# Both layer norms' linear part in TensorE's moving matrix, and three experts on the first half of the tokens ahead of the second

## The reference

```
# layer 0, per token; W, b, emb are picked by the sample's domain id
hidden = gelu(x @ down_W.T + down_b)                   # 32 wide
hidden = hidden @ expert_W[id].T + expert_b[id] + domain_emb[id]
x = layernorm(hidden @ up_W.T + up_b + x) * ln_gamma + ln_beta
# layer 1
h = layernorm(x) * ln_g + ln_b                         # over the features
h = (h - mean over tokens) * rsqrt(var over tokens + 1e-8)
gamma, beta = style(subject id)                        # four small products, softplus
h = h * gamma + beta
gates = the two largest of softmax(h @ router_w), normalised    # 8 experts
y = sum over e of gate_e * (relu(h @ w1_e + b1_e) @ w2_e + b2_e)  # 512 wide
out = x + y
```

## Time and profile before

| | |
|---|---|
| runs | 126.09, 122.81, 125.94 us; median 125.94 |
| profiled execution | 122.93 us; span of its instructions 121.1 us |
| TensorE busy | 114.2 us (94%), 515 matmuls |
| VectorE busy | 93.1 us (77%) |
| ACT busy | 86.6 us (71%) |
| POOL busy | 54.3 us (45%) |
| first expert product | 21.24 us |
| last expert product | 115.41 us |

### The profile page before, as it was taken

One profiled execution on the slowest core, in us unless ns is written; L12 is line 12 of the kernel. 1 busy time (PEld: TensorE's weight loads), 2 busy tenths in 40 slices (PEclk: granted clock), 3 DMA queues, 4 the chain that ended last, 5 costly groups with the idle time before them and its releaser, 6 DMA issues.

```text
span 121.1 us, 1653 instructions
## 1 busy us (share of the span) xinstructions
PE 114.2 (94%) x515; PEld 86.5 (71%) x515; DVE 93.1 (77%) x238; ACT 86.6 (71%) x147; POOL 54.3 (45%) x75
## 2 busy tenths in 40 slices
PE   6999889999859999999999999999999999999990
PEld 2557533888548888788888888888888888888780
DVE  4756999999996699895867777685959577776871
ACT  2157596589789996978778787878787876878300
POOL 5200986420594001100089997948577940312300
PEclk9999756999999999999999999999999999999999
DMA  1998599990000005065999100000000000000006
GB/s 64 374 221 341 138 438 449 349 349 16 0 3 0 0 0 173 8 184 133 345 431 425 54 0 0 5 0 0 0 0 0 0 0 0 5 0 0 0 0 173
DMA packets 4328, 14.17 MB, mean 117 GB/s; under 512 B 544, under 2 KB 1888, under 8 KB 4064
## 3 DMA queue, kind: packets, MB, share of 16 engines
q1 hardware_dynamic: 2880, 9.67, 22.4%
q0 software_dynamic: 1008, 3.67, 8.9%
q10 hardware_dynamic: 432, 0.73, 1.7%
HBM read 13.52 MB, written 0.56 MB: 116 GB/s over the span
## 4 chain that ended last, share of the span: by engine, by line
PE 73%; DVE 21%; issue 2%; ACT 1%
PE bank L577 21%; PE bank L578 20%; PE bank L616 11%; PE bank L596 11%; PE bank L621 4%; DVE hid_low L990 3%; DVE x L887 2%; DVE h_full L969 2%; DVE stats L894 1%; DVE h_low L975 1%; DVE z L931 1%; PE bank L548 1%; DVE bank L879 1%; DVE t_stats L915 1%; DVE stats L846 1%
## 5 line engine op out<-in xcount | busy, mean ns | idle before, releaser
L491 ACT ACTIVATE hid_high<-bank,early_sb 128x512 fp32r<-128x512 f32 x64 | 44.3, 692 | 16.1 <-PE bank L596 16.0
L990 DVE TENSOR_TENSOR hid_low<-bank,hid_high 128x512 fp32r<-128x512 f32 x51 | 34.6, 687 | 18.8 <-ACT bank L494 18.3
L494 ACT ACTIVATE bank<-bank,early_sb 128x512 f32<-128x512 f32 x51 | 33.5, 658 | 0.0
L301 POOL TENSOR_TENSOR w_low<-w_raw,w_high 128x256 fp32r<-128x256 f32 x32 | 23.0, 743 | 12.1 <-ACT w_high L479 6.1
L616 PE MATMUL bank<-hid_low,w_high 128*128 128x512 f32 x64 | 25.6, 399 | 1.5 <-DVE hid_low L990 1.3
L577 PE MATMUL bank<-h_high,w_low 128*128 128x512 f32 x64 | 25.6, 400 | 0.7 <-ACT h_high L473 0.7
L577 PE MATMUL bank<-hid_high,w_low 128*128 128x512 f32 x64 | 25.7, 402 | 0.0
L578 PE MATMUL bank<-h_high,w_high 128*128 128x512 f32 x64 | 25.3, 396 | 0.0
L596 PE MATMUL bank<-h_low,w_high 128*128 128x512 f32 x64 | 25.1, 394 | 0.0
L578 PE MATMUL bank<-hid_high,w_high 128*128 128x512 f32 x64 | 25.0, 391 | 0.0
L311 POOL TENSOR_TENSOR y_sum<-y_sum,y_part 128x512 f32<-128x512 f32 x9 | 11.6, 1291 | 19.0 <-DVE y_part L1010 16.9
(11 more groups left out here) (136 smaller groups left out, 110.3 us busy)
## 6 DMA issues: line engine op xcount, KB each, us to landing
w_high<-w_all_dram POOLq DMA_DIRECT2D x7, 512.0 KB, 6.9
w_raw<-w_all_dram SPq DMA_DIRECT2D x1, 3072.0 KB, 10.9
gate_all<-gate_scratch SPq DMA_DIRECT2D x4, 512.0 KB, 5.5
gate_all<-gate_scratch SPq DMA_DIRECT2D x1, 2048.0 KB, 11.4
w_raw<-w_all_dram SPq DMA_DIRECT2D x2, 512.0 KB, 7.8
style_sb<-style_dram SPq DMA_DIRECT2D x1, 324.0 KB, 4.8
tables_sb<-tables_dram ACTq DMA_DIRECT2D x1, 272.0 KB, 3.0
xT_sb<-xT_dram SPq DMA_DIRECT2D x1, 256.0 KB, 3.6
```

Source lines behind the costliest of these rows:

```text
L301: nc.gpsimd.tensor_tensor(w_low[:, e % W_RING, quarter(q)], w_raw[:, e, quarter(q)], w_high[:, e % W_RING, quarter(q)].bitcast(F32), ALU.s ...
L491: ac(hid_high[:, slot, :], hid_ps[slot][:, :], ACT.Relu, bias=bias).then_inc(relu_steps, 1)
L494: ac(hid_ps[slot][:, :], hid_ps[slot][:, :], ACT.Relu, bias=bias).then_inc(relu_steps, 1)
L990: v.tensor_tensor(low, ps, high.bitcast(F32), ALU.subtract).then_inc(low_vector, 1)
```

## The change

The moving matrix of `residual` and `up` becomes 256 wide (`moments`). Its first 127 columns give a vector whose squares add up to 128 times the variance of the sum; column 127 gives the covariance with beta; the last 128 give the centred sum times gamma. So a sum comes out of PSUM centred and scaled. ACT squares and adds up the first part (`energies`), VectorE takes statistics of the last part and works out from both, in small steps of one column a tile, what the variance of the second norm will be (`sum_var`, `token_var`), without the finished x1. One pass (`shifted`) adds beta times the root. The second norm reads that; x1 itself is made by POOL later (`adapter_out`).

The matrix is built on the chip: POOL makes its constant parts and puts gamma, beta and the up bias, loaded as columns, on diagonals; TensorE multiplies, ACT copies. The up matrix is transposed, multiplied by `moments` (`build_up`) and then by the selected expert (`adapter`), a half at a time, and VectorE copies it (`take_adapter`).

For half 1 POOL takes the roots as powers. ACT loads one table less for Sqrt and one less for Exp; `w_high` of expert 0 comes by a load and not from ACT. POOL normalises one tile each of samples 0 and 1 and both of samples 2 and 3; the statistics over tokens stay with VectorE. Expert 2 on half 0 stands ahead of half 1, so 12 units do instead of 8; the gates are transposed at unit 20 instead of 18. The warm products change from 10 at the start and 5, 6, 3, 2 in the head to 6, 2 and 6, 2, 2.

Of the order lists the new order is shown; the old one stands in the functions above.

```diff
-PRE_ORDER = [(0, 0), (1, 0), (0, 1), (1, 1), (2, 0), (2, 1)]
-WARM_LOAD, WARM_NORM = 10, (5, 6, 3, 2)
-FEATURE_ROOT = 4
+PRE_ORDER = [(0, 0), (1, 0), (2, 0), (0, 1), (1, 1), (2, 1)]
+SECOND = PRE_ORDER.index((0, 1)) * FC
+WARM_LOAD, WARM_BUILD, WARM_NORM = 6, 2, (6, 2, 2)
...
+            sp.dma_start(ln0_cols[:, :], ln_row.rearrange("a b d -> d (a b)"), allow_slow_non_contiguous=True
+                         ).then_inc(ln0_cols_loaded, 16)
             sp.dma_start(xT_sb[:, 0:HN], xT[:, 0:HN]).then_inc(x_loaded[0], 16)
+            up_b_at = EARLY.at["up_b"][0]
+            sp.dma_start(up_b_col[:, :], early[A:A + 1, up_b_at:up_b_at + D].rearrange("a d -> d a"),
+                         allow_slow_non_contiguous=True).then_inc(up_b_loaded, 16)
+            sp.dma_start(xT_sb[:, HN:N], xT[:, HN:N]).then_inc(x_loaded[1], 16)
+            sp.dma_start(style_sb[:, 0:STYLE_FIRST], style[:, 0:STYLE_FIRST]).then_inc(style_loaded, 16)
...
+            sp.dma_start(w_raw[:, 2, :], w_all[:, 2, :]).then_inc(w_loaded[2], 16)
+            sp.dma_start(w_raw[:, 3:E, :], w_all[:, 3:E, :]).then_inc(w_loaded[3], 16)
...
+            pool.wait_ge(ln0_cols_loaded, 16)
+            nc.gpsimd.tensor_scalar(gain_rows[:, 1:1 + D], ident[:, :], ln0_cols[:, 0:1], None, ALU.mult
+                                    ).then_inc(gain_rows_ready, 1)
+            nc.gpsimd.tensor_scalar(gain_rows[:, 0:1], ln0_cols[:, 1:2], ln0_cols[:, 0:1], 1.0 / D, ALU.mult, ALU.mult
+                                    ).then_inc(gain_rows_ready, 1)
+            pool.wait_ge(up_b_loaded, 16)
+            for b in range(HB):
+                nc.gpsimd.tensor_copy(up_b_rows[:, b * SLOT + A:b * SLOT + A + 1], up_b_col[:, :]).then_inc(up_b_ready, 1)
...
+            def normalise(b, tiles):
+                pool.wait_ge(sum_taken, T * (b + 1))
+                pool.wait_ge(mean1_ready, b + 1)
+                if b < HB:
+                    pool.wait_ge(rstd1_ready, b + 1)
+                else:
+                    pool.wait_ge(rstd1_power, b - HB + 1)
+                for j in (b * T + t for t in tiles):
+                    nc.gpsimd.tensor_scalar(z[:, j, :], x1_std[:, j, :], mean1[:, j:j + 1], rstd1[:, j:j + 1],
+                                            ALU.subtract, ALU.mult).then_inc(z_pool, 1)
...
+            def token_rstd(b):
+                js = slice(b * T, (b + 1) * T)
+                pool.wait_ge(var1_ready, b + 1)
+                nc.gpsimd.tensor_tensor(rstd1[:, js], var1[:, js], roots_of[:, 1, :], ALU.pow).then_inc(rstd1_power, 1)
...
+            load_high(0)
             load_high(1)
-            split_lows(0)
-            normalise(0)
-            split_lows(1, (0, 1))
+            normalise(0, (1,))
+            normalise(1, (1,))
+            split_lows(0, (0, 1))
+            pool.wait_ge(pool_steps, steps.n)
+            feature_rstd(0)
+            split_lows(0, (2, 3))
             load_high(2)
             load_high(3)
-            pool.wait_ge(affine_ready, HB)
+            sum_std(2)
+            sum_std(3)
+            token_rstd(2)
+            normalise(2, range(T))
+            split_lows(1, (0, 1))
+            token_rstd(3)
+            normalise(3, range(T))
             split_lows(1, (2, 3))
             load_high(4)
             load_high(5)
-            normalise(2)
-            for q in POOL_UNITS:
-                split_hidden(q)
+            split_lows(2, (0, 1))
+            feature_rstd(1)
+            split_lows(2, (2, 3))
             pool.wait_ge(affine_ready, B)
-            split_lows(2)
             split_lows(3)
+            adapter_out()
...
+            act.dma_start(ids_i[:, :], ids).then_inc(ids_loaded, 16)
             act.dma_start(tables_sb[:, :, :], tables).then_inc(tables_loaded, 16)
             act.dma_start(early_sb[:, :], early).then_inc(early_loaded, 16)
-            act.dma_start(xT_sb[:, HN:N], xT[:, HN:N]).then_inc(x_loaded[1], 16)
...
+            ac(moments[:, K_DIFF:2 * D], gain_ps, ACT.Copy).then_inc(gain_ready, 1)
+            act.wait_ge(up_T_in_psum, 1)
+            ac(up_T[:, :], up_T_ps, ACT.Copy).then_inc(up_T_ready, 1)
+            act.wait_ge(up_moments_in_psum, 1)
+            ac(up_moments[:, :], up_moments_ps, ACT.Copy).then_inc(up_moments_ready, 1)
...
+                    act.wait_ge(sum_in_psum, j + 1)
+                    if b >= HB:
+                        act.wait_ge(stats_ready, T * (b + 1))
+                    elif t > 0:
+                        act.wait_ge(stats_ready, T * b + 1)
+                    ac(z[:, j, 0:K_DIFF], sum_ps[j][:, 0:K_DIFF], ACT.Square, accum_out=energy[:, j:j + 1]
+                       ).then_inc(energy_ready, 1)
...
+            energies(0)
+            sum_std(0)
             act.wait_ge(style_in_psum, 4)
             ac(sty1_T[:, :], sty1_ps, ACT.Relu, bias=col(C_SB1, SC)).then_inc(style_ready, 1)
+            energies(1)
+            token_std(0)
+            sum_std(1)
             act.wait_ge(style_in_psum, 6)
             ac(gamma_raw[:, :], gam_ps, ACT.Identity, bias=col(C_SBG)).then_inc(gamma_beta_ready, 1)
             ac(beta_T[:, :], bet_ps, ACT.Identity, bias=col(C_SBB)).then_inc(gamma_beta_ready, 1)
+            token_std(1)
             softplus()
+            energies(2)
+            energies(3)
             round_h(0)
+            for q in range(9):
+                relu_unit(q)
             round_h(1)
...
+            build_gain()
+            warm(WARM_BUILD, misc[1])
+            up_bias(0)
+            transpose_up()
+            down(0)
+            build_up()
+            down(1)
+            down(2)
+            down(3)
+            adapter(0)
             residual(0)
+            up(0)
+            up_bias(1)
+            adapter(1)
             mm(se_ps, STYLE.of(style_sb, "subj", SUBJ), onehot_s[:, :], start=True, stop=True).then_inc(style_in_psum, 1)
             residual(1)
             up(1)
...
             residual(2)
             pe.wait_ge(style_ready, 2)
+            up(2)
             pe.wait_ge(style_ready, 3)
+            residual(3)
+            pe.wait_ge(style_end_loaded, 16)
             pe.wait_ge(style_ready, 4)
             transpose_z(0)
+            up(3)
             pe.wait_ge(soft_in, 1)
             transpose_z(1)
+            warm(WARM_NORM[0], bank[3])
+            pe.wait_ge(t_rstd_ready, 1)
+            warm(WARM_NORM[1], bank[3], S)
+            pe.wait_ge(affine_ready, HB)
             warm(WARM_NORM[2], bank[3], S)
+            pe.wait_ge(h_even_rounded, 1)
+            pe.wait_ge(h_odd_rounded, 1)
...
+            for q in range(3):
                 first_highs(q)
             pe.wait_ge(h_ready, 1)
+            for q in range(3):
                 first_low(q)
             first_product(3)
+            second_product(0)
+            first_product(4)
             pe.wait_ge(sum_taken, T * HB + T)
             router(0)
+            second_product(1)
             first_product(5)
+            second_product(2)
+            first_product(6)
+            second_product(3, between=lambda: transpose_z(2))
+            first_product(7)
+            second_product(4)
+            first_product(8)
             transpose_z(3)
+            second_product(5)
+            for q in range(9, SECOND):
                 first_product(q)
                 second_product(q - LEAD)
+            def first_of_second_half():
+                pe.wait_ge(h_even_rounded, HALVES)
+                pe.wait_ge(h_odd_rounded, HALVES)
+                first_highs(SECOND)
+            second_product(SECOND - LEAD, between=first_of_second_half)
             pe.wait_ge(h_ready, HALVES)
...
+            def take_adapter(h):
+                ve.wait_ge(up_eff_in_psum, h + 1)
+                v.tensor_copy(up_eff[:, h, :], up_eff_ps[:, h, :]).then_inc(up_eff_ready, 1)
...
+            def sum_var(b):
+                last = v.tensor_scalar(var0[:, js], energy[:, js], 1.0 / D, LN_EPS, ALU.mult, ALU.add)
+                if b < HB:
                     last.then_inc(vec_steps, steps.add())
+                    own()
                 else:
+                    last.then_inc(var0_ready, 1)
+                    own()
+                    ve.wait_ge(var0_ready, b - HB + 1)
                 for j in tiles(b):
+                    v.scalar_tensor_tensor(cov[:, j:j + 1], mv[:, j, 0:1], minus_shift[:, 0:1], sum_ps[j][:, K_DIFF:K_SHARE],
+                                           ALU.mult, ALU.add).then_inc(vec_steps, steps.add())
+                v.scalar_tensor_tensor(var_share[:, js], var0[:, js], shift_var[:, 0:1], mv[:, js, 1], ALU.mult, ALU.add
+                                       ).then_inc(vec_steps, steps.add())
+                mark["share", b] = steps.n
...
+            def token_var(b):
+                js = slice(b * T, (b + 1) * T)
+                after(("share", b))
+                if b < HB:
+                    ve.wait_ge(std0_ready, b + 1)
+                else:
+                    ve.wait_ge(std0_power, b - HB + 1)
```

(61 more changed lines are left out.)

541 lines of the change are left out of this document (235 added, 306 removed).

## The result

The changed kernel takes 136.2 us (median of 136.0, 136.41, 137.14 and 134.48) where the kernel before took 125.1 beside it: ratio 1.098, 95% interval 1.072 to 1.123. Slower was right. The size was not: 129.5 was forecast, and the range ended at 133.0. The profiled execution took 136.0 us with a span of 134.3, against 122.93 and 121.1 before. All ratios in this document leave out the runs of either kernel that lie more than 1.5% above its fastest one on that chip, so that they can differ from the quotient of the medians.

The account below looks back on a forecast made before the run. TensorE's expert products (89.4 us that can't shrink) were taken to bound the kernel, leaving the 21.24 us head and 2.07 us of stalls in reach; 122.93 + 3.8 (head) + 2.8 (stalls) = 129.5 us, range 125.5 to 133.0.

Parts of the forecast that it names:

- The head: Everything ahead of the first expert product: that product at 25.0 instead of 21.24, +3.8 us.
- The bias column: Load at the head's front: lands near 4.8, with POOL's masks waiting behind it until 5.8.
- Scale and shift: Last VectorE steps of the head before rounding, after softplus and offset end at 24.05: 0.35 us.
- Unit 4's wait: First product of unit 4 waits for expert 1's low weights, late in POOL's line: 2.4 us.
- rival 1: Clock returns from 1.2 GHz only after the first expert product, doubling product times: 131.0 to 132.6 us, chance 0.18.
- The second half: Stalls from VectorE's work on the second half of the tokens: 0.8 at unit 5 and 1.0 before h_ready(2).
- The stall at unit 5: Second product of unit 5 waits for VectorE, which has feature_stats(3) before split_unit(5): 0.8 us.
- the later parts: After the stage: cost nothing, though POOL's expert 4 quarter has little cover left and may cost up to 0.5 us.
- rival 2: Shorter front, cheap POOL line: first statistic at 11, first expert product at 23.2, stalls 2.1; 124.9 us, chance 0.14.
- 3: VectorE's passes alone bound head and stage; first expert product at 20.4, 2.07 us stall gone; 120.1 us, chance 0.08.
- Rival 4: Stage keeps its stall despite four more units: 2 us more at the second half, 131.5 us, chance 0.08.
- The table load: Removed load back to Sqrt in the head: worth nothing; by the skill's drain rule 1.2 us, forecast 128.3.

Follow-up runs that it names:

- Experiment 11: Changed kernel with one more wait on POOL: expert 0's third and fourth low quarters wait for the first half's scale and shift; 137.9 us, ratio 1.101.
- experiment 7: Kernel of experiment 6 with the adapter's second copy, style steps and ACT's root of sample 1 reordered in the head; 131.2 us, runs 128.1 to 133.4.
- experiment 1: Changed kernel with POOL making expert 1's first two low quarters right after expert 0's; 134.3 us, ratio 1.080.
- Experiment 2: Changed kernel with sixteen bf16 products of zeros on TensorE ahead of unit 4; 133.7 us, ratio 1.075.
- second kernel of experiment 11: Changed kernel with that POOL wait, expert 1's first quarters earlier, the second half normalised on VectorE, five products of zeros at the start; 130.0 us, ratio 1.038.
- experiment 4: Changed kernel with style steps moved behind sample 0's small steps on VectorE and sty1's copy behind sample 1's squares on ACT; 137.4 us, ratio 1.094.
- 8: Kernel before with only the second part of the change: three experts on the first half ahead of the second half, old norms; 122.3 us, ratio 0.992.
- 3: Kernel of experiment 1 with the second half's normalising moved from POOL to VectorE; 132.2 us, ratio 1.064.
- experiment 6: Kernel of 5 with ten instead of two products of zeros before the scale and three instead of two after it; 133.2 us, ratio 1.076.
- experiment 12: Second kernel of experiment 11 with the head's order changed on VectorE and ACT; 128.7 us, ratio 1.049.
- 13: Kernel of 8 repeated: 122.4 us, ratio 0.997; then with sample 3's transposes and the gates' last passes moved later: 123.1 us, ratio 1.000.
- 5: Changed kernel with six low quarters ahead of POOL's first normalise and the second half normalised on VectorE; 131.0 us, ratio 1.060.
- 9: Changed kernel once more with no edit; 137.3 us, ratio 1.086.

## Why the prediction was wrong

**The head, +3.8 forecast, +5.5 measured.** The first statistic was forecast at 12.5 and came at 13.18. The bias column was late: issued at 1.78, it landed 3.9 us later, at 5.7 and not near 4.8. But that isn't where the 0.7 come from. The sum has the bias product end at 6.8, "still at 1.2 GHz"; the trace has it end at 6.86 after 0.67 us for the pair, with a granted clock of 1.00, as it also reads over the first products of the kernel before. `build_up` then starts at 7.45, just as in the sum. Behind it each of the eight 256-column products took 0.48 to 0.62 from start to start where 0.45 was taken, and that is the 0.7. The mechanism was as told, with take_adapter(1) ahead of the first statistic.

The order of the waits behind it was as told too: hyp1_T at 15.14 (forecast 14.15), sty1's copy at 17.54 (16.8), the square of tile 2 right behind it. A square shows as two rows, 0.26 to 0.28 and then 0.19 or 0.20, but two squares with both rows took 0.50 (17.70 to 18.20), less than the 0.7 of the sum. VectorE's statistics end at 22.97 (22.6) and the offset at 24.45 (24.05), so the head was 0.4 late up to here.

The term that was mis-sized worst is the last. Scale and shift stand in the sum with 0.35, and from the offset's end to the shift's it took 1.54: the gain, which is in no term, took 0.57, the scale 0.65 and the shift 0.34. POOL's power did hide, as the sum has it. What stretched the gain and the scale were POOL's quarters at 24.31 to 25.7. Experiment 11 shows 0.16 each without them and 0.9 us less from statistic to product. So the step that failed here is the price of POOL's line: the sum prices it by what TensorE waits for, never by what VectorE loses beside it. The profile of the kernel before had a warning. It has the same two passes of h_low twice, first beside no more than the tail of a quarter (20.03 to 21.43), then beside POOL's eight quarters of 31.63 to 37.56:

```profile
21.03 1.02 DVE L975 TENSOR_TENSOR h_low<-h_full,h_high 128x256 fp32r<-128x256 f32 x2
...
32.63 1.58 DVE L975 TENSOR_TENSOR h_low<-h_full,h_high 128x256 fp32r<-128x256 f32 x2
```

The Trainium skill (SBUF — State Buffer, SBUF: two separate sides) says that a GpSimd instruction that reads SBUF and a VectorE instruction with two SBUF inputs shut each other out for a whole instruction. By that rule, the trace agrees: 0.65 is nearly a quarter's 0.70, and the passes that read PSUM kept their length. The page adds VectorE's two-port modes; the pass with one input that took 0.62 in experiment 7 may be of that kind, which no row here shows.

**Unit 4's wait, +2.4 forecast, 3.3 measured.** Place, cause and the chain in front of it were right, and experiment 1 shows it to be POOL's order. What was short is POOL's two normalising passes, 1.58 with the new form (subtract, multiply) where I took 0.87 from a row with multiply and add: 0.7 of the 0.9.

**The step that failed:** the units behind that wait were priced at full clock, 0.233 a product. Of the clock the forecast asked only whether it comes back late after the head (rival 1); it never asked what its own stall of 2.4 us in the middle of the units would do to it, though the profile of before has such a fall after a sparse stretch. It cost 3.3 us. Experiment 2 (the wait kept, the engine fed: the clock stays up) and the second kernel of experiment 11 (the wait taken away: the clock stays up) show it from both sides, and in all five profiles with the 3.0 us gap unfilled the clock falls in the last 1.7 us of the gap or less than 1 us behind it. Of the 6.5 us by which the profiled execution passed the forecast, the clock has 3.3, the head 1.7 and the stalls 1.5.

**Rival 1** was right as a mechanism and wrong in its place. In the changed kernel the clock was back before the first product. In experiments 4 and 8 it was down over the first products, and in 1 and 3 it fell some 0.5 to 1 us behind the first one. In those two the gap at unit 4 was gone, and TensorE had been idle for 1.8 and 2.0 us, but for two small products of zeros, just ahead of the first product; that this is the cause was not tested, since experiment 6 failed to.

**The second half, +1.8 forecast in its two places.** The stall at unit 5 was 0.8, as forecast; the later ones 1.0, 0.25 and 0.4, against 1.0. The whole of the stalls was 4.7 in the forecast and 6.4 in the trace, and 0.9 of the difference is unit 4's. That the later parts cost nothing was right.

**Rivals 2 and 3** fell with the first statistic; the products of 33 rows, for which rival 2 hoped, took as long as those of 128 (1.13 us for four instructions of either). **Rival 4** had 2 us more at the second half; it was 0.7. The table load played no part that a run shows, and neither did the 1.38 us of drain that the prediction weighs: in the changed kernel a load starts at 10.40, takes 1.28, and the next activation starts at 11.70.

**What was right:** that the first part of the change costs the head more than it saves VectorE. In the best order tried it is still 3.7 us (experiment 12), and the second part without the first costs nothing and may gain up to 1% (experiments 8 and 13).

## What to carry to other kernels

Where a change makes a tensor engine wait for microseconds in the middle of its products, add to the wait what the next units cost at half clock, and try the wait filled with idle products before anything else. When work moves between engines, count the small passes as well as the columns: here the saved passes of 128 columns became two-column passes, each of which a neighbour's pass can stretch from 0.16 to 0.65 us. Move a neighbour's work by what runs beside it, not only by when its engine is idle.

## What was unexpected of the hardware

- TensorE's first products run at one of two speeds for up to some 7 us: 0.67 or 1.19 for the same pair of bias products at 6.2, 0.70 or 1.22 for the next. The granted clock reads 1.00 in both. With the slow start the adapter's first copy stands at 11.3 to 13.0 instead of 9.6 to 10.2. Between experiment 2 and the changed kernel, with the same head, it moves the first expert product by 3.6 us (30.37 and 26.74). What decides it was not found: it stands in four of the ten profiles with two products of zeros ahead of the bias product, and in none of the three with five, which are too few to tell.
- The clock's fall lasted from some 3 us (experiment 4, in the head) to some 10 (experiments 5 and 9).
- An activation that accumulates along its row shows as two instructions: 0.26 to 0.28 and then 0.19 to 0.22.
- POOL's power of 128 rows and two columns takes 0.69 to 0.73 us; its tensor_scalar of 128x128 takes 0.79 with subtract and multiply, 0.60 with multiply alone, and took 0.44 with multiply and add before.
